# Four comparison blocks of a second pass move from VectorE to GpSimd in two mixture stages

## The reference

```python
x = x + 0.5 * mixture64(layernorm(x))      # f0
x = x + attention0(layernorm(x))           # a0
x = x + 0.5 * mixture64(layernorm(x))      # g0, same weights as f0
x = x + 0.5 * mixture8(layernorm(x))       # f1
x = x + attention1(layernorm(x))           # a1
x = x + 0.5 * mixture8(layernorm(x))       # g1, same weights as f1
```

```python
probs = softmax(x @ router_w.T)
topk_w, topk_ids = top_k(probs, K);  topk_w /= topk_w.sum(-1)
flat_e = topk_ids.reshape(-1)
pos = number of earlier choices of the same expert
valid = pos < C                              # only the first 64 tokens of an expert
xb = tokens gathered into [E, C, 128]
y = (silu(xb @ w_gate) * (xb @ w_up)) @ w_down
routed = segment_sum(y of each valid choice * its weight, token)
shared = silu(x @ sg) * (x @ su) @ ws_down   # one expert for every token
result = routed + shared
```

## Time and profile before

| | us |
|---|---|
| median of 3 runs | 1003.87 (1003.46 to 1012.12) |
| the profiled execution | 1006.11 |
| its span, first to last instruction | 1004.4 |
| busy in the span: PE | 843.0 (84%) |
| DVE | 715.2 (71%) |
| ACT | 547.4 (55%) |
| POOL | 292.1 (29%) |

### The profile page before, as it was taken

How to read it: one execution, slowest core, us unless ns; L and a number is a source line. 1 busy time by engine, 2 the same in 40 slices (tenths; PEclk the granted TensorE clock), 3 DMA queues, 4 the chain that set the end, 5 groups by cost and what they waited for, 6 DMA issues and landing times.

```text
span 1004.4 us, 23032 instructions
## 1 busy us (share of the span) xinstructions
PE 843.0 (84%) x7234; PEld 633.2 (63%) x7238; DVE 715.2 (71%) x2557; ACT 547.4 (55%) x1498; POOL 292.1 (29%) x423
## 2 busy tenths in 40 slices
PE   5889987899986899948699288999999998659992
PEld 4357854466654357836699255677767766548992
DVE  7757888477757866886556658877787788467555
ACT  4233043578774223014467438877887888435664
POOL 2034125834201002117755270000000000057771
PEclk9999996799996999976989779999999999959997
DMA  8208951112106204053540246554646462163413
GB/s 253 61 0 285 383 203 44 44 45 78 55 4 165 80 0 143 1 153 105 160 108 32 89 147 189 159 159 128 189 129 182 127 196 86 28 198 85 116 41 128
DMA packets 135459, 119.99 MB, mean 119 GB/s; under 512 B 11012, under 2 KB 115740, under 8 KB 135349
## 3 DMA queue, kind: packets, MB, share of 16 engines
q1 hardware_dynamic: 130804, 110.09, 36.6%
q0 software_dynamic: 4544, 8.54, 2.4%
HBM read 67.45 MB, written 51.80 MB: 119 GB/s over the span
## 4 chain that ended last, share of the span: by engine, by line
PE 61%; DVE 14%; ACT 12%; issue 5%; DMA 3%; SPq 2%; POOL 1%; DVEq 1%; POOLq 0%; ACTq 0%
PE psum L1596 6%; PE psum L964 6%; PE psum L973 6%; PE psum L1510 5%; PE psum L2808 4%; PE psum L2260 3%; PE psum L2857 3%; PE psum L2188 3%; ACT a_L L2938 3%; ACT a_L L2936 3%; PE psum L2844 2%; PE psum L741 2%; PE psum L1536 2%; PE psum L2824 2%; DVE a_negmax L2442 2%
## 5 line engine op out<-in xcount | busy, mean ns | idle before, releaser
L2442 DVE TENSOR_REDUCE a_negmax<-psum 128x2 f32<-128x512 f32 x128 | 83.1, 688 | 35.8 <-PE psum L2188 32.7
L2388 ACT ACTIVATE a_PT<-psum 128x1024 f32<-128x1024 f32 x64 | 64.9, 1020 | 13.3 <-PE psum L2197 12.9
L2938 ACT ACTIVATE a_L<-a_L,a_least 128x256 f32<-128x256 f32 x128 | 63.3, 495 | 0.0
L2808 PE MATMUL psum<-a_KT,a_Q 64*128 64x128 f32 (+1 forms) x512 | 57.6, 342 | 3.4 <-DVE a_least L2998 1.1
L1021 ACT ACTIVATE g_hT<-psum,g_wt 128x128 f32<-128x128 f32 x156 | 44.5, 368 | 24.3 <-PE psum L964 24.3
L1021 ACT ACTIVATE f_hT<-psum,f_wt 128x128 f32<-128x128 f32 x156 | 44.5, 368 | 22.0 <-PE psum L964 22.0
L2936 ACT ACTIVATE a_L<-a_L,a_least 128x128 f32<-128x128 f32 x128 | 50.6, 395 | 10.7 <-DVE a_least L2998 9.8
L2996 DVE CUSTOM_DVE_ANT_0 a_L<-psum,a_X 128x128 f32<-128x128 f32 x128 | 36.8, 287 | 25.0 <-PE psum L2808 24.9
L2998 DVE CUSTOM_DVE_ANT_0 a_L<-psum,a_X 128x256 f32<-128x256 f32 x128 | 53.8, 421 | 0.0
L2947 ACT ACTIVATE a_PT<-psum 128x768 f32<-128x768 f32 x64 | 51.2, 799 | 1.5 <-PE psum L2824 0.7
L2824 PEld LDWEIGHTS psum<-ident,a_L 64*128 64x128 f32 x768 | 30.3, 138 | 30.5 <-ACT a_PT L2947 17.5
(11 more groups left out here) (588 smaller groups left out, 2493.8 us busy)
## 6 DMA issues: line engine op xcount, KB each, us to landing
z<-a_G SPq DMA_DIRECT2D x32, 512.0 KB, 3.5
a_X<-z SPq DMA_DIRECT2D x16, 1024.0 KB, 6.7
f_slots_dram<-empty SPq DMA_DIRECT2D x1, 8910.0 KB, 29.2
g_slots_dram<-empty SPq DMA_DIRECT2D x1, 8910.0 KB, 51.9
a_X<-z SPq DMA_DIRECT2D x16, 512.0 KB, 4.1
f_wgu<-in_gate_up SPq DMA_DIRECT2D x16, 384.0 KB, 6.4
z<-pad SPq DMA_DIRECT2D x6, 1024.0 KB, 5.4
g_wgu<-in_gate_up SPq DMA_DIRECT2D x16, 384.0 KB, 6.5
```

The lines of the kernel that those rows point to most:

```text
L2388: act.activation(PT[m % 4][:, :, :, :].rearrange("p j t n -> p j (t n)"), core.psum[:, 2 + 2 * (u % 2):4 + 2 * (u % 2), :], ACT.Exp, scale ...
L2442: dve.tensor_reduce(negmax[:, :, h], query_bank(b, h).rearrange("p (t n) -> p t n", n=SEQ), AX.X, ALU.max, negate=True).then_inc(max_done, 1)
L2808: last = pe.matmul(out, Q[rows, at, b % 2, queries], KT[rows, at, b % 2, keys], start=True, stop=True)
L2938: act.activation(pr[:, o, P:3 * P], L[:, o, P:3 * P], ACT.Exp, bias=least[:, o, 1:2], scale=-1.0, accum_out=sums[:, o, 1:2]).then_inc(p_re ...
```

## The change

GpSimd, after its last subtraction and the iota, makes the first four blocks of pass 1, in the order of the counts `combined` 29 to 32. VectorE's loop makes blocks 4 to 31 only and then goes on to the additions into x; at the loop's start it waits for `c_made` to reach 4 (round 0), or 36 (round 1). `own_token` has two planes in place of three, and VectorE fills two. GpSimd makes its four blocks whatever `passes` is.

```diff
     PASS = 8
     PASSES = TILES // PASS
-    own_token = sb("own_token", [P, PASSES + 1, PAIRS])
+    assert PASSES == 2
+    own_token = sb("own_token", [P, PASSES, PAIRS])
...
                 pool.iota(pass_token, [[1, PASS * P]], base=1, channel_multiplier=0,
                           allow_small_or_imprecise_dtypes=True).then_inc(numbered, 1)
+        for p in range(RING):
+            pool.wait_ge(combined, PAIRS - RING + p + 1)
+            pool.tensor_scalar(ST[:, p, :].bitcast(F32R), pass_token, own_token[:, 1, p:p + 1], None,
+                               ALU.is_equal).then_inc(c_made, 1)
...
-        for t in range(PASSES + 1):
+        for t in range(PASSES):
             dve.tensor_scalar(own_token[:, t, :], of_slot[:, :, 4], float(-P * PASS * t), None, ALU.add)
...
         with dve.Fori(0, passes) as t:
-            for p in range(RING, PAIRS + RING):
+            dve.wait_ge(c_made, t * PAIRS + RING)
+            for p in range(RING, PAIRS):
                 dve.wait_ge(combined, t * PAIRS + (p - RING + 1))
-                ahead = p // PAIRS
                 dve.tensor_scalar(ST[:, p % RING, :].bitcast(F32R), pass_token,
-                                  own_token[:, ds(t + ahead, 1), p % PAIRS], None, ALU.is_equal).then_inc(c_made, 1)
+                                  own_token[:, ds(t, 1), p], None, ALU.is_equal).then_inc(c_made, 1)
```

## The result

| | before | with the change |
|---|---|---|
| first comparison, median of 4 runs each | 1003.99 (1003.46 to 1012.12) | 1021.09 (1017.66 to 1026.14) |
| its ratio, 95% interval | | 1.0139 (1.0089 to 1.0189) |
| second comparison (experiment e5) | 1006.68, 23 runs | 1020.60, 4 runs |
| its ratio, 95% interval | | 1.0139 (1.0125 to 1.0154) |
| profiled execution, its span | 1004.4 | 1024.4 |

The forecast was 1018 with a range of 1004.5 to 1037. The four runs of the first comparison fall in two pairs, 1017.7 and 1017.9, 1024.3 and 1026.1; the profiled one is the longest of them, so its span overstates the difference. The second comparison, 13.9 us, is the better measure.

What follows compares the result with a forecast made beforehand. The prediction took the last engine to reach the barrier ending f0 and g0 as the bound. Two ends 7.0 us later (+14.0), less 0.3 for own_token, gave 1003.9 + 13.7 = 1017.6, rounded to 1018; range 1004.5 to 1037.

Steps and rivals of the forecast that it cites:

- What bounds the stage end: At the ends of f0 and g0, the later of VectorE and GpSimd moves everything behind the barrier one for one.
- T: GpSimd's time for one 128x1024 comparison with a scalar of each partition: 2.94 us taken, break-even 1.19 us.
- the constant-scalar row: Profile row of GpSimd TENSOR_SCALAR, one operation and a constant: 518 ns at 128 elements, extrapolated to 2.94 us at 1024.
- the two-scalar row: Profile row of GpSimd TENSOR_SCALAR, two operations, two per-partition scalars: 785 ns at 128 elements, extrapolated to 5.27 us.
- the forecast's row: The GpSimd one-operation, constant-scalar TENSOR_SCALAR row chosen for the forecast: 2.71 ns an element, 2.94 us a block, chance 0.42.
- the upper rival: GpSimd's blocks: the scalar from SBUF is the cost, 5.27 us each, +32.4 us, total 1036; chance 0.28.
- The sum: Ends of f0 and g0: GpSimd's four blocks at 2.94 us end each stage 7.0 us later, together +14.0 us.
- VectorE's gain: At each of the two stage ends, VectorE's adds start and end 0.9 us earlier without the four blocks.
- own_token: Losing one of three small VectorE instructions in the chain of f0 and g0 saves 0.3 us together.
- The clock: TensorE's granted clock at the starts of a0 and f1: already at half level, so nothing added, bound 1 us.
- Edits at nothing: VectorE's added loop wait, adds beside GpSimd's blocks, clock and DMA cost nothing; contention stretching GpSimd at most 2.15 us a stage.
- The copy's pace: Rival: GpSimd compares as fast as it copies, 1.06 us a block, -1.3 us, total 1002.5; chance 0.12.

Runs made afterwards that it cites:

- e5: The changed kernel run again unaltered, against the kernel before on the same chip: 1020.60 us against 1006.68, ratio 1.0139.
- e1: Changed kernel, but GpSimd makes its four blocks only if passes is over 1; 1046.96 us against 1048.32 for the kernel before, ratio 1.0002.
- e3: Changed kernel, with GpSimd making its four blocks and then the same four again; 1081.77 us against 1048.32 for the kernel before, ratio 1.0320.
- e4: Changed kernel, with each stage's four GpSimd blocks replaced by other, unread GpSimd instructions to price them; one-operation TENSOR_SCALAR with a constant 2783 ns; no total given.
- e6: The kernel before against itself, nothing changed: 1005.91 us against 1006.68, ratio 0.9987.
- e8: Changed kernel plus 40 filler matmuls on TensorE after its last transposes of f0 and g0; 1019.85 us against 1006.68 for the kernel before, ratio 1.0124.
- e2: Changed kernel with two blocks on GpSimd, two on VectorE, three-plane own_token and no added loop wait; 1052.15 us against 1048.32 for the kernel before, ratio 1.0041.
- e9: Changed kernel with one block on GpSimd, three on VectorE, otherwise like the two-and-two split; 1008.60 us against 1008.15 for the kernel before, ratio 1.0012.
- e7: The kernel whose GpSimd blocks are made only if passes is over 1, run again; 1005.36 us against 1006.68 for the kernel before, ratio 0.9993.

## Why the prediction was right

**What bounds the stage end: right.** The prediction said that the stage ends with the later of VectorE and GpSimd and that this moves everything behind it one for one. e1 takes the blocks away and the whole cost goes; e3 doubles them and each end comes later by their 11.27 us.

**T: right, with a reason that was half wrong.** 2.94 us was taken, 2.84 measured. I chose the constant-scalar row over the two-scalar row because the latter has twice the slope with twice the operations. The choice was right (e4: the scalar from SBUF adds 0.06 us), but two operations cost 1.33 times one, not twice. What went wrong is the extrapolation from 128 elements. The 12-element row of 204 ns, from which three of the four slopes start, is L710, an instruction with two operations, and it lies below the line of the larger ones. The slopes taken from it are too steep, 5.0 ns where 3786 and the earlier trace rows's 785 give (3786 - 785) / 896 = 3.35, and 2.71 where e4's 2783 and 518 give 2.53. For the forecast's row the error was 6% (2.94 against 2.78), 4% against the comparison itself; for the upper rival it was 40% (5.27 against 3.79).

**The sum: 7.0 us a stage forecast, 6.29 measured.** T gives 4 x 0.10 = 0.4 of the difference, GpSimd's start 0.1 (at -1.09, I had -0.99), and the barrier the rest: from GpSimd's last end to the next stage 0.14 us, where VectorE's took 0.31. That the total still came within 0.2 us of the forecast (13.9 measured, 13.7 forecast) is in part luck: the two stage ends were put 1.4 us too high, and 1.7 us that nothing here explains make up for it.

**VectorE's gain: right in size, and worth nothing.** 0.9 us was forecast, 0.8 measured; GpSimd's end hides it. e1 lays it bare.

**own_token:** 0.3 us forecast; 0.2 in the instructions, 0.4 with the gap in f0 that went with it.

**The clock: right for the start of a0, open behind it.** It was forecast at nothing with a bound of 1 us, from the half level at both stage starts. That level isn't there in every execution (e6 begins a0 at the full clock), but no run shows a cost of either: a0 takes 174.9 us after a start at half and 177.9 after one at full with the kernel before, 177.6 and 177.9 with the change (e5, e8). Further into a0 the clock does matter, and the prediction had nothing for that beyond its 1 us. The long a0 was seen twice, with 182.5 us in the first profile of the change and 182.4 in e3. In these two TensorE's granted clock is at the half level for 58 us of a0 in all, in the ten other profiles for 37 to 44. At 41.2 us into a0 VectorE starts the same instruction, its 115th, in the first profile and in e5; its 134th starts at 62.5 us in the one and at 57.5 in the other, and the 5 us stay to the end. Between the two lie these windows (the clock is again the third figure from the end), of the first profile:

```profile
185.00:190.00 5.00, 4.38 (x30) 2.36 (x30) 2.37 (x7) 2.24 (x4) 5.00 (x7) 0.50 0.01 3
190.00:195.00 5.00, 4.78 (x34) 3.04 (x38) 2.83 (x6) 2.66 (x4) 4.77 (x9) 0.50 0.11 32
```

and of e5:

```profile
185.00:190.00 5.00, 3.83 (x44) 2.24 (x43) 2.96 (x6) 3.35 (x6) 5.00 (x7) 1.00 0.01 3
190.00:195.00 5.00, 3.76 (x40) 2.29 (x34) 3.19 (x8) 3.30 (x5) 4.77 (x10) 1.00 0.51 144
```

The long a0 came in two of the eight profiles in which blocks on GpSimd make the stage end longer, and in none of the four of the kernel before and of e1's. That is too few to say whether the change makes it likelier.

**Edits at nothing.** The added wait at VectorE's loop shows no cost (e1 has it, and its time is that of the kernel before). Contention between VectorE and GpSimd was costed only for the adds, where none shows: they take 2.16 us beside GpSimd's blocks and 2.15 alone. With comparison blocks on both sides (e2, e9) it is real.

**The rivals.** The copy's pace was excluded by 2.84 against 1.19. The Trainium skill, GPSIMD Engine Reference, section 4.1 (Engine selection), which calls one-input work roughly line-rate, agrees with e4's copy (1042 ns) and not with its five one-input TENSOR_SCALAR instructions of that width, 2.78 to 3.79 us.

**Open.** 1.7 us between the stage ends with own_token (12.2) and the median (13.9). Each a0 and g1 varies by 3 us and more from run to run, and four runs of the change stand against 23 of before. What keeps TensorE at the half clock 14 us and more longer in some executions of a0, and why g_xin sometimes lands 1.5 us later, wasn't found.

## What to carry to other kernels

An idle engine at the end of a stage is not free capacity if a barrier follows: what counts is when its share ends against the engine that ended the stage until now, here 4.76 us of room for 11.3 us of work. Price a moved instruction by its own kind at its own size, since on GpSimd a copy, an addition of a tensor to itself and an operation with one scalar of one shape differ by up to 2.7 times. And work made ahead for a pass that may not come belongs behind a test of whether it comes: that took the loss away (e1, e7).

## What the runs showed of the hardware

- GpSimd, 128x1024 f32: copy 1.04 us, tensor added to itself 1.89, TENSOR_SCALAR with one operation 2.78 to 2.85, with two 3.65 to 3.79; the source of the scalar matters by 0.06 to 0.14.
- VectorE's and GpSimd's comparison blocks slow each other without shutting each other out: in e9 VectorE's first two blocks began and ended inside GpSimd's one instruction. The three took 1.15 us more than alone and the one 0.37. In e2 VectorE's two kept their 0.75 us inside GpSimd's first, which took 0.45 more.
- TensorE idle for 9.1 us enters a0 at the half clock (0.50), and with fillers at the full one (1.00), with no effect on a0's length that shows (177.6 and 177.9 us).
- Within a0 the same instructions took 4 to 8 us longer where TensorE's granted clock was at the half level for 58 us in all and not for 37 to 44 (182.5 and 182.4 us against 174.7 to 177.9).
- The same kernel takes 1004 to 1008 us in three of the comparisons and 1048 us on the chip of e1 to e4; most of the difference lies in the two 8-expert stages (in e1, f1 154.8 and g1 154.8 us, against 136.3 and 130.4).
